# A perceiver block on one core: two small products turned into transposes, seven zero matmuls taken out of the heads, and a sum over keys split between two engines

## The reference

```python
a  = softmax(ctx @ ln(x).T, axis=-1)        # over the 128 queries
x  = x + a.T @ ctx
# 16 heads of 16, causal
q, k, v = split(ln(x) @ w_attn + b_attn)
p  = softmax(mask(q @ k.T / 4), axis=-1)
x  = x + concat_heads(p @ v) @ w_proj + b_proj
x  = x + ln(x) @ W.T + b + (ln(x) @ V_r) @ C.T
```

## Time and profile before

| | us |
|---|---|
| median of three runs | 107.9 (106.49 to 108.13) |
| the profiled execution, its own time | 106.67 |
| its span, first to last instruction | 104.6 |
| end of the last context product on PE | about 84.6 |
| start of the first transpose of exponentials | 93.25 |
| start of the projection | 98.64 |
| end of the last DVE instruction | 102.45 |

### The profile page before, as it was taken

One profiled execution on the slowest core, in us unless ns is written; L12 is line 12 of the kernel. 1 busy time (PEld: TensorE's weight loads), 2 busy tenths in 40 slices (PEclk: granted clock), 3 DMA queues, 4 the chain that ended last, 5 costly groups with the idle time before them and its releaser, 6 DMA issues.

```text
span 104.6 us, 2280 instructions
## 1 busy us (share of the span) xinstructions
PE 100.0 (96%) x749; PEld 87.7 (84%) x749; DVE 75.9 (73%) x216; ACT 72.6 (69%) x268; POOL 65.1 (62%) x51
## 2 busy tenths in 40 slices
PE   6999999999999999999999999999999999999990
PEld 1288999999999999999999999999998976857760
DVE  0411849979999999788777797777799646696741
ACT  4018499799999999987777977778879205399310
POOL 6404499979999999998666697666795010017020
PEclk9999999999999999999999999999999999999998
DMA  2999999999999999999999999992000000000001
GB/s 72 351 389 415 415 412 407 404 410 406 412 403 406 409 406 414 409 409 417 395 414 407 404 411 403 386 334 73 0 0 6 0 0 0 0 0 0 6 0 50
DMA packets 8746, 27.86 MB, mean 266 GB/s; under 512 B 1120, under 2 KB 1824, under 8 KB 8736
## 3 DMA queue, kind: packets, MB, share of 16 engines
q1 hardware_dynamic: 8736, 27.73, 67.7%
HBM read 27.59 MB, written 0.13 MB: 265 GB/s over the span
## 4 chain that ended last, share of the span: by engine, by line
PE 86%; DMA 7%; ACT 2%; SPq 2%; DVE 1%; issue 1%
PE bank L330 39%; PE bank L342 20%; PE bank L345 10%; DMA cols_ring<-ctx_cols_dram 7%; PE bank L410 2%; PE bank L435 1%; ACT head_exp L581 1%; PE bank L351 1%; PE bank L445 1%; PE bank L423 1%; PE bank L507 1%; PE bank L493 1%; PE bank L393 1%; PE bank L390 1%; SPq L228 1%; PE bank L464 1%
## 5 line engine op out<-in xcount | busy, mean ns | idle before, releaser
L289 POOL TENSOR_TENSOR rows_split<-rows_ring,rows_split 128x1024 fp32r<-128x1024 f32 (+1 forms) x25 | 58.4, 2338 | 17.4 <-ACT rows_split L525 17.4
L330 PE MATMUL bank<-query_t,cols_ring 128*128 128x128 f32 x392 | 47.8, 276 | 0.4 <-ACT query_t L516 0.2
L330 PEld LDWEIGHTS bank<-query_t,cols_ring 128*128 128x128 f32 x392 | 45.7, 192 | 1.9 <-DMA cols_ring<-ctx_cols_dram 0.6
L536 ACT ACTIVATE bank<-bank,neg_max 128x128 f32<-128x128 f32 x98 | 33.0, 337 | 8.0 <-DVE neg_max L660 7.8
L342 PE MATMUL bank<-rows_split,probs 128*128 128x512 f32 x92 | 34.7, 413 | 0.0
L525 ACT CAST rows_split<-rows_ring 128x1024 fp32r<-128x1024 f32 (+1 forms) x25 | 25.8, 1033 | 6.1 <-DMA rows_ring<-ctx_rows_dram 5.0
L677 DVE SCALAR_TENSOR_TENSOR probs<-bank,inv_sums,probs 128x128 fp32r<-128x128 f32 x98 | 27.7, 345 | 0.9
L345 PE MATMUL bank<-rows_split,probs 128*128 128x256 f32 x92 | 25.6, 279 | 0.0
L660 DVE TENSOR_REDUCE neg_max<-bank 128x4 f32<-128x512 f32 (+1 forms) x25 | 16.8, 672 | 9.0 <-PE bank L330 9.0
L342 PEld LDWEIGHTS bank<-rows_split,probs 128*128 128x128 f32 x92 | 17.3, 189 | 3.1
L536 ACT ACTIVATION_READ_ACCUMULATOR bank<-bank,neg_max 128x1 f32 x98 | 19.8, 202 | 0.0
(11 more groups left out here) (96 smaller groups left out, 65.3 us busy)
## 6 DMA issues: line engine op xcount, KB each, us to landing
cols_ring<-ctx_cols_dram SPq DMA_DIRECT2D x24, 512.0 KB, 14.3
rows_ring<-ctx_rows_dram SPq DMA_DIRECT2D x24, 512.0 KB, 14.9
wqk_sb<-w_qk_dram SPq DMA_DIRECT2D x1, 512.0 KB, 11.0
cols_ring<-ctx_cols_dram SPq DMA_DIRECT2D x1, 256.0 KB, 10.9
rows_ring<-ctx_rows_dram SPq DMA_DIRECT2D x1, 256.0 KB, 11.6
wv_sb<-w_v_dram SPq DMA_DIRECT2D x1, 256.0 KB, 11.6
wproj_sb<-w_proj_dram SPq DMA_DIRECT2D x1, 256.0 KB, 10.5
wffn_sb<-w_ffn_dram SPq DMA_DIRECT2D x1, 256.0 KB, 9.6
```

The costliest lines, as they stand in the source:

```text
L289: pool.tensor_tensor(rows_split[:, b, 0:n, 1, :], rows_ring[:, slot * STEP:slot * STEP + n, :], rows_split[:, b, 0:n, 0, :].bitcast(F32), ...
L330: last = pe.matmul(into[:, t * P:(t + 1) * P], cols_ring[:, slot * STEP + t, c, :], query_t[:, c, :], start=(c == 0), stop=(c == DC - 1))
L536: last = act.activation(on[:, t * P:(t + 1) * P], on[:, t * P:(t + 1) * P], ACT.Exp, bias=neg_max[:, b, t:t + 1], accum_out=sums[:, b, t:t ...
```

## The change

- `spread_inverse` is issued as a transpose (one pass) instead of a float32 matmul with the identity.
- The two products that put the centred residual into `x2_t_ps` become transposes and move from behind `turn_exps(1)` to straight after the values; the product into `x2_ps` stays where it was, and now waits for `v_copied`, since it has taken over the values' bank.
- `turn_exps`, the inverse sums, `x2_ps`, `x2_t_ps` and `ffn_ps` sit in other banks.
- The zero matmuls in the heads (5 and 2 of 512 columns) are gone; at the start two of 256 columns are added, one ahead of the first transposes and one behind them. `keep_warm` writes to bank 7 now.
- POOL halves group 1 twice instead of seven times, and DVE adds the remaining 32 columns up with one reduction.
- `project_turned(0, 0)` stands ahead of the wait for `inv_copied_end`.

```diff
-        exp_t_ps = [bank[5], bank[6], bank[7]]
-        exp_t_ends = [bank[5], bank[6]]
-        inv_ps = [bank[2][:, P:2 * P], bank[1][:, P:2 * P]]
+        exp_t_ps = [bank[5], bank[0], bank[1]]
+        exp_t_ends = [bank[5], bank[0]]
+        inv_ps = [bank[7][:, P:2 * P], bank[6][:, P:2 * P]]
         y_t_ps = [bank[3], bank[4]]
-        x2_ps, x2_t_ps, ffn_ps = bank[0], [bank[1], bank[2]], bank[6]
+        x2_ps, x2_t_ps, ffn_ps = bank[2], [bank[7], bank[6]], bank[1]
...
-        WARM_START, WARM_X, WARM_EXPS, WARM_TURN = 4, 2, 5, 2
+        WARM_START, WARM_X = 4, 2
...
-            width, folds = P // 4, 1
-            while width > 1:
-                pool.wait_ge(fold_step, folds)
-                pool.tensor_tensor(folded[:, :, 0:width], folded[:, :, 0:width], folded[:, :, width:2 * width],
-                                   ALU.add).then_inc(fold_step, 1)
-                width, folds = width // 2, folds + 1
-            pool.wait_ge(fold_step, folds)
-            pool.tensor_tensor(head_sums[:, 0, 1, :].unsqueeze(2), folded[:, :, 0:1], folded[:, :, 1:2], ALU.add)\
-                .then_inc(sums_folded, 1)
+            pool.wait_ge(fold_step, 1)
+            pool.tensor_tensor(folded[:, :, 0:P // 4], folded[:, :, 0:P // 4], folded[:, :, P // 4:P // 2], ALU.add)\
+                .then_inc(fold_step, 1)
...
-            def keep_warm(count, into=turn[0][:]):
+            def keep_warm(count, into=scores[3], width=4):
...
             keep_warm(WARM_X)
+            keep_warm(1, width=2)
             turn_normed(0)
+            keep_warm(1, width=2)
...
-            keep_warm(WARM_EXPS, exp_t_ps[0][:])
+            pe.wait_ge(x1_bias_centred_ready, 1)
+            for c in range(DC):
+                pe.transpose(x2_t_ps[c][:, 0:P], x1_bias_centred[:, c * P:(c + 1) * P], ident[:])
...
                 pe.matmul(inv_ps[c], head_inv_wide[:, c].rearrange("p m e d -> p (m e d)"), ident[:],
-                          start=False, stop=True, skip_group_check=True).then_inc(inv_spread, 1)
+                          start=False, stop=True, is_transpose=True, skip_group_check=True).then_inc(inv_spread, 1)
...
             turn_exps(0)
-            keep_warm(WARM_TURN, exp_t_ps[1][:])
             turn_exps(1)
+            pe.wait_ge(v_copied, 2)
             pe.matmul(x2_ps[:, 0:D], ident[:], x1_bias[:], start=True, stop=False, skip_group_check=True)
-            pe.wait_ge(x1_bias_centred_ready, 1)
-            pe.wait_ge(v_copied, 2)
-            for c in range(DC):
-                pe.matmul(x2_t_ps[c][:, 0:P], x1_bias_centred[:, c * P:(c + 1) * P], ident[:], start=True, stop=False,
-                          skip_group_check=True)
...
             project(0)
+            project_turned(0, 0)
             pe.wait_ge(inv_copied_end, 1)
-            project_turned(0, 0)
             project_turned(1, 0)
...
-            dve.wait_ge(sums_folded, 1)
+            dve.wait_ge(fold_step, 2)
+            link(dve.tensor_reduce(head_sums[:, 0, 1, :], folded[:, :, 0:P // 4], AX_X, ALU.add))
             invert_sums(0)
```

More of the change, by code:

```diff
@@ L185, in perceiver_kernel @@
         fold_step = sem("fold_step")
-        sums_folded = sem("sums_folded")
         exp_turned = sem("exp_turned")
@@ L356, in weigh @@
                 last.then_inc(summed, 1)
-            def keep_warm(count, into=turn[0][:]):
+            def keep_warm(count, into=scores[3], width=4):
                 for _ in range(count):
-                    pe.matmul(into, warm[:], warm[:].unsqueeze(1).to_broadcast([P, 4, P]), start=True, stop=True)
+                    pe.matmul(into[:, 0:width * P], warm[:], warm[:].unsqueeze(1).to_broadcast([P, width, P]),
+                              start=True, stop=True)
             def mask_scores(j):
```

## The result

| | before | changed |
|---|---|---|
| median of six runs, us | 107.19 (106.3 to 108.13) | 105.68 (105.5 to 105.9) |
| profiled execution, its own time | 106.67 | 105.76 |
| its span | 104.6 | 103.7 |
| from the q and k products' start to DVE's last start | 14.27 | 13.81 |

The ratio to the kernel before is 0.9943, 95% interval 0.9921 to 0.9964, about 0.6 us, less than the 1.5 us between the medians. The runs of the kernel before come in two sorts, 105.8 to 107.0 and 107.6 to 108.3, those of the changed kernel only in the faster one, and the ratio compares the faster ones alone.

What follows compares the result with a forecast made beforehand. In the heads PE was taken to bound the kernel, its queue meeting ACT or POOL, then DVE, at the projection. The 0.44 us gained there, all else 0, off 107.3 gave 106.9 us, range 105.6 to 108.5.

Steps and rivals of the forecast that it cites:

- Part 1: PE between the turns: zero matmuls and residual products removed, 0.88 us, of which 0.48 gained by the last half turn.
- Part 2: Inverse sums spread as transposes: half the products' time, 0.30 to 0.38 us off PE's queue; DVE bounds there.
- Part 3: Sums on POOL and DVE: DVE's reduction takes about 0.32 us, and DVE is free at 96.94, before at 97.51.
- Part 4: Where PE's and DVE's chains meet: the projection starts 0.4 to 0.5 us earlier, 0.44 taken.
- Part 5: Projection onward, the moved wait, other banks and ACT: nothing else changes, 0.
- Part 6: Start of the kernel: the two added zero matmuls of 256 columns cost 0 in all.
- The sum: Whole kernel: 0.44 us off the path, from the middle of four known times, 107.3, to 106.9 us.
- the better start: Rival, chance 0.10: added matmuls at the start help slower runs reach full clock, worth up to 1.5 us: 105.5 to 106.0.
- The fallen clock: Rival, chance 0.13: TensorE's clock falls in the heads without the zero matmuls; 109.8 us if from the projection on.

Runs made afterwards that it cites:

- experiment 4: Changed kernel with the five and the two zero matmuls put back at their old places in the heads; ratio 0.9965 to the kernel before.
- experiment 8: Changed kernel with the residual's transposes as two float32 products behind the turn of group 1; ratio 1.0 to the kernel before, median 106.46 us.
- experiment 6: Changed kernel with the inverse sums spread by float32 products again, run twice; ratio 0.9962 to the kernel before.
- Experiment 7: Changed kernel with all seven halvings on POOL and no reduction on DVE; ratio 0.9997 to the kernel before, median 106.46 us.
- experiment 9: Changed kernel with PE's second half turn and first spread ahead of the second product with the values; ratio 0.9957 to the kernel before.
- Experiment 11: Changed kernel with 72 float32 transposes of the identity added ahead of the projection; these took 8.02 us.
- experiment 2: Kernel before with only the two zero matmuls of 256 columns added at the start; twelve runs at 106.05 to 106.93 us, ratio 1.0019.
- experiment 1: Kernel before, unchanged, run again; eight runs at 105.99 to 106.85 us, four at 107.74 to 108.27.
- experiment 3: Changed kernel without the two added zero matmuls at the start; nine runs at 105.54 to 106.47 us, three at 107.52 to 107.86, ratio 0.9967.
- experiment 5: Changed kernel, unchanged, run again; twelve runs at 105.54 to 106.20 us, ratio 0.9964 to the kernel before.

## Why the prediction was right, and where its median was off

- **Part 1** (PE between the turns): the turn of group 2 was forecast at 95.18, less the 0.45 of the earlier start 94.73, and came at 94.72. The gain of 0.48 did not come. It was taken against 95.66, the place of the turn in the chain, which is where the record before has drained; in the timeline, where the 95.18 belongs, the turn started at 95.49. Group 2 and the last half turn, first before, then changed:

```profile
95.49 0.60 PE L435 MATMUL bank<-ident,head_exp 128*128 128x128 f32 x4
...
97.10 0.44 PE L464 MATMUL bank<-ident,head_exp 128*128 128x128 f32 x2
```

```profile
94.72 0.66 PE L433 MATMUL bank<-ident,head_exp 128*128 128x128 f32 x4
...
96.39 0.44 PE L462 MATMUL bank<-ident,head_exp 128*128 128x128 f32 x2
```

  Less the 0.45, the gain is 0.32 at the turn and 0.26 at the last half turn, since the turn, now behind a wait, takes 0.59 to the next start (95.31) and before took 0.53 (to 96.02). That group 2 is what PE waits for was right. Of the 0.88 counted as removed, the zeros' 0.43 only made room for the new wait for v's copy (experiments 4 and 8); the residual's products are worth 0.38 (experiment 8).
- **Part 2** (spreads): the pair takes half, as said, and is worth 0.08 in the stretch. That DVE holds the end there is right for the kernel with products (experiment 6); PE's own saving of 0.23 goes into its wait for ACT's copy of the last half, which the forecast had as "in time".
- **Part 3** (sums): the reduction took 0.28, I took 0.32 between 0.20 and 0.68; DVE was free for its last copy at 96.48, forecast 96.94 - 0.45 = 96.49. Experiment 7 confirms that chain with 0.40.
- **Part 4** (where the two meet): 0.44 forecast, 0.46 in the stretch, in part by luck. DVE's side came as forecast: first y at 97.59, forecast 97.99 - 0.45 = 97.54, and 1.53 after ACT's last exponential, forecast 1.5. PE's side did not: it was to be through with the values at 97.93 - 0.45 = 97.48, ahead of y, and its next product, the projection's, starts at 97.74. Of these 0.26, 0.19 are the wait for ACT's copy (0.76 for 0.57). That hardly moved the sum, because the forecast had let DVE decide and both arrive within a few hundredths: the projection's first product starts 0.15 after the first y ends in the changed kernel (97.59 to 97.74), and as much in experiments 6 and 7, where y is late. By experiments 9 and 11 it is PE's queue that is last, by very little. In PE's chain the gain is 0.26 (part 1) and 0.39 (the spreads' 0.60 less the 0.21 that now lies between the last half turn and the values), less the 0.19: 0.46. The 0.48 of part 1 did no harm, since the forecast reached the end through times of the timeline and not through that gain.
- **Part 5** (nothing else): the projection behind has the same pieces, 0.63 and 0.44. The exchange of banks was not free, it brought the wait for v's copy; its price stands in part 1.
- **Part 6** (the start, "0 in all"): this step failed. For the profiled execution and for the faster runs it is right (experiment 2, 1.0019). For the median it is not: the kernel before reaches full speed late in some of its launches. Over all launches, four far ones left out (166.05, 201.61, 254.56, 548.95), 42 of 116 without the added zeros (the kernel before and experiments 1 and 3) lay at 107.5 or above, and none of 89 with them (the changed kernel and experiments 2, 4 to 9). I had it as a rival at 0.10, with the right mechanism, and dismissed it because the profiled execution showed no loss; but a profiled execution is one launch, and was one of the faster.
- **The sum**: 106.9 was the middle of both sorts less 0.44. The faster sort alone, 106.3 to 106.7, less 0.44, would have given 105.9 to 106.2. The range held 105.68 only because it reached to the better start.
- **The fallen clock**: did not come. In the changed kernel PE stands idle for 1.00 ahead of the turn of group 0, and the granted clock stays 1.00. Experiment 11 excludes that 8 us of transposes alone bring it down. Longer waits of PE in the heads were not tried.

Open: the faster runs of one kernel still spread over 0.4 to 1.1 us. In the trace of experiment 1 the two zero matmuls ahead of x took 0.77 together, in that of the kernel before 1.06, so full speed came at different moments there too. That this makes all of the spread was not shown. Why 512 added columns are enough was not tried either: neither one of the two alone, nor another size.

## What to carry to other kernels

When two engines' chains meet at one point, find out for each what it alone would give: here either half alone gained under 0.1 us and both together 0.46. Take both ends of a gain from the same view: the chain and the timeline place one instruction up to 0.17 apart. When a few runs fall into two groups, ask what differs between launches before forecasting from their middle, and look at the first microseconds. A stand-in for work (the zeros in the heads) may be without effect once something else waits in its place, and another of the same kind (at the start) may be worth more, in the launches that it helps, than all the rest of the change.

## What the runs showed of the hardware

- The granted clock column reads 1.00 from the start of the trace while PE issues at half its later rate. Six float32 score records a microsecond against eleven is the sign to look for.
- A launch can run at the lower level until about 10 us (experiment 3), while another whose program starts with the same instructions is at full speed at 5.5 us (experiment 1).
- 72 float32 transposes of 128 columns on a clock at full level: 0.111 us each, granted clock 1.00, full speed behind them.
- A group of PE instructions behind a semaphore wait often starts after 0.17 to 0.22 us in which its weight loads stand idle, put down to "issue". It shows at changes between transposes and products with the values, and also between two groups of such products (0.22 at 97.35 in the changed kernel); from the spreads to the values in experiment 6 there is none. What sets it is not shown.
- One execution had a mean granted clock of 0.571, in 164.0 us of span: 0.8 or more in the first two of 40 slices, about half in all later ones. Another of the same kernel took 548.95 us at a granted clock of 1.0. What brought either there is not known.
